# First attention of a four-layer model: order of scores and maxima products, place of the second batch's output turn, and six score banks in the last group

## The reference, cut to what matters

```python
qkv = jnp.einsum('bsd,od->bso', x, w_project)          # 16 heads of 16 features
att = jnp.einsum('bhqd,bhkd->bhqk', q, k) / math.sqrt(HEAD_DIM)
att = jnp.where(causal, -1e9, att)
att = jax.nn.softmax(att, axis=-1)
out = jnp.einsum('bhqk,bhkd->bhqd', att, v)
return jnp.einsum('bsd,od->bso', out.reshape(b, s, d), w_out)
```

## Time and profile before

| | |
|---|---|
| time, median of three runs | 1347.25 us |
| the profiled execution, its own time | 1347.06 us |
| its span | 1345.3 us |
| PE busy | 1225.4 us, 91% of the span |
| DVE busy | 731.3 us, 54% |
| ACT busy | 605.4 us, 45% |
| POOL busy | 121.5 us, 9% |
| first attention, first score to output projection | 85.65 to 182.60 us |

### The profile page before, as it was taken

How to read it: one execution, slowest core, us unless ns; L and a number is a source line. 1 busy time by engine, 2 the same in 40 slices (tenths; PEclk the granted TensorE clock), 3 DMA queues, 4 the chain that set the end, 5 groups by cost and what they waited for, 6 DMA issues and landing times.

```text
span 1345.3 us, 18762 instructions
## 1 busy us (share of the span) xinstructions
PE 1225.4 (91%) x6396; PEld 765.1 (57%) x6396; DVE 731.3 (54%) x2031; ACT 605.4 (45%) x1518; POOL 121.5 (9%) x144
## 2 busy tenths in 40 slices
PE   5988888888899889999999899999999999999994
PEld 4644444523277455656565687566666666667853
DVE  2777626836142578787878710444444444447257
ACT  2634553787623134545455402444545444442043
POOL 3230013432301300000000000000000000000000
PEclk9979999999999989999999999999999999999998
DMA  8001100230232400000000002100000000000000
GB/s 242 6 18 32 43 28 0 93 83 20 75 97 90 171 12 12 12 13 13 9 9 8 1 0 75 67 24 12 25 13 23 20 17 20 17 12 1 1 0 31
DMA packets 28046, 48.66 MB, mean 36 GB/s; under 512 B 3902, under 2 KB 22302, under 8 KB 26886
## 3 DMA queue, kind: packets, MB, share of 16 engines
q1 hardware_dynamic: 25222, 38.13, 8.8%
q0 software_dynamic: 2736, 9.37, 2.4%
HBM read 40.36 MB, written 9.19 MB: 37 GB/s over the span
## 4 chain that ended last, share of the span: by engine, by line
PE 69%; DVE 13%; issue 10%; ACT 7%; POOL 1%; DMA 0%; SPq 0%; ACTq 0%; POOLq 0%; DVEq 0%
PE bank L977 13%; PE bank L993 9%; PE bank L984 8%; PE bank L962 5%; PE bank L970 5%; PE bank L988 4%; PE bank L1223 2%; PE bank L886 2%; PE bank L897 2%; ACT PT L1487 2%; PE bank L1314 2%; PE bank L1274 2%; PE bank L1241 2%; PE bank L816 1%; PE bank L1301 1%
## 5 line engine op out<-in xcount | busy, mean ns | idle before, releaser
L1368 ACT COPY R<-bank 128x512 f32<-128x512 f32 (+4 forms) x199 | 106.3, 550 | 314.7 <-PE bank L993 142.8
L2064 DVE CUSTOM_DVE_ANT_0 bank<-bank,mask_row 128x128 f32<-128x128 f32 (+3 forms) x256 | 126.9, 497 | 173.4 <-PE bank L984 171.0
L977 PE MATMUL bank<-XNT,W 128*128 128x512 f32 x416 | 201.4, 608 | 7.4 <-ACT R L1368 3.8
L1515 ACT ACTIVATE R<-bank,nm 128x128 f32<-128x128 f32 (+3 forms) x256 | 136.0, 531 | 111.1 <-DVE nm L2064 110.1
L984 PE MATMUL bank<-R 128*128 128x512 f32 (+3 forms) x384 | 134.3, 434 | 0.0
L977 PEld LDWEIGHTS bank<-XNT,W 128*128 128x128 f32 x416 | 75.4, 192 | 101.9 <-issue 93.1
L962 PE MATMUL bank<-W,R 128*128 128x256 f32 x576 | 125.3, 380 | 3.2 <-ACT R L1368 3.2
L962 PEld LDWEIGHTS bank<-W,R 128*128 128x128 f32 x576 | 109.1, 190 | 18.7 <-ACT R L1368 2.1
L988 PE MATMUL bank<-identf,R 128*128 128x128 f32 x640 | 112.4, 275 | 6.3 <-DVE R L2081 4.7
L993 PE MATMUL bank<-PT,R 128*128 128x128 f32 (+3 forms) x384 | 112.0, 435 | 5.6 <-ACT PT L1368 4.2
L1368 ACT COPY PT<-bank 128x128 f32<-128x128 f32 (+3 forms) x256 | 108.6, 426 | 15.3 <-PE bank L988 15.1
(11 more groups left out here) (278 smaller groups left out, 1815.0 us busy)
## 6 DMA issues: line engine op xcount, KB each, us to landing
W<-in_wq SPq DMA_DIRECT2D x32, 128.0 KB, 2.0
W<-in_wo SPq DMA_DIRECT2D x2, 2048.0 KB
W<-in_egu SPq DMA_DIRECT2D x1, 2816.0 KB
W<-in_wk SPq DMA_DIRECT2D x20, 128.0 KB, 2.1
W<-in_wv SPq DMA_DIRECT2D x20, 128.0 KB, 2.0
R<-xg SPq DMA_DIRECT2D x5, 512.0 KB, 4.6
yg<-R SPq DMA_DIRECT2D x5, 512.0 KB, 3.5
W<-in_wa SPq DMA_DIRECT2D x2, 1024.0 KB, 4.7
```

What stands on the lines that cost most here:

```text
L977: ins = mm(bank[:, :], wqkv23[:, s, c, :], XNT[:, c, b * SEQ:(b + 1) * SEQ], start=c == 0, stop=c == DC - 1)
L1368: return nc.scalar.copy(dst, src)
L1515: return fn(Pr[c][:, 0:n], PS[c][:, 0:n], ACT.Exp, scale=-1.0, bias=nm[:, c:c + 1], accum_out=esum[:, c:c + 1])
L2064: return dve.tensor_tensor_reduce(out=s[:, 0:n], in0=s[:, 0:n], in1=mask_row[:, SEQ - n:SEQ], scale=-1.0, scalar=-MASKED, op0=ALU.add, op1 ...
```

## The change

Scores are no longer issued step by step but by number up to a limit, `scores(upto)`. In groups 0 to 2, step w issues three heads of step w + 1, then maxima tiles 0 and 1, then the fourth head. The output turn of a group's second batch moves from the group's end to step 0 of the next group, behind the fourth head's scores (for group 2 to step 1 of the last group), and DVE's normalisation moves with it. Only the last group's own second batch is still turned at the end. In the last group the scores from step 1 on use six banks, 3, 5, 7, 1, 2, 0 in turn: the first three wait for the last reduction of the maxima, the others for the exponential six scores before. The turn of the last maxima moves to step 0 behind the scores, and ACT copies them ahead of the exponentials of step 1 instead of step 2.

```diff
--- before.py
+++ after.py
@@ -323,6 +323,12 @@
         OUT_BANK, TURN_BANK = 4, 6
         MAX_BANKS = (3, 5, 7)
 
+        LAST0 = ((NG - 1) * B * TPB + 1) * GH
+        LAST_BANKS = (3, 5, 7, 1, 2, 0)
+
+        def score_bank0(n):
+            return n % 3 if n < LAST0 else LAST_BANKS[(n - LAST0) % 6]
+
 
         KV3_STEPS = {1: ("q", 0), 3: ("k", 0), 4: ("v", 0), 5: ("q", 1), 6: ("k", 1), 7: ("v", 1)}
         TILES = B * TPB
@@ -792,18 +798,26 @@
                 cb = coreb[0]
                 rows, stages = KQ + 3, B * TPB
 
-                def scores(g, w):
-                    b, j = w // TPB % B, w % TPB
-                    if j == 0:
-                        pe.wait_ge(nm_row[b], 64 * (g + 1 + B))
-                    q0 = j * P
-                    for h in range(GH):
-                        n = (g * stages + w) * GH + h
-                        pe.wait_ge(cb["pb_ready"], n + 1 + GH - 3)
-                        dst = PS[n % 3]
+                issued = [0]
+
+                def scores(upto):
+                    for n in range(issued[0], upto):
+                        g, w, h = n // (stages * GH), n // GH % stages, n % GH
+                        b, j = w // TPB, w % TPB
+                        if j == 0 and h == 0:
+                            pe.wait_ge(nm_row[b], 64 * (g + 1 + B))
+                        q0 = j * P
+                        if n < LAST0:
+                            pe.wait_ge(cb["pb_ready"], n + 1 + GH - 3)
+                        elif n < LAST0 + 3:
+                            pe.wait_ge(smax_used, NG * stages * TPB + 2)
+                        else:
+                            pe.wait_ge(cb["pb_ready"], n + 1 + GH - 6)
+                        dst = PS[score_bank0(n)]
                         mm(dst[:, q0:SEQ], kstk[0:rows, g * GH + h, b * SEQ + j * P:b * SEQ + (j + 1) * P],
                            qstk[0:rows, g * GH + h, b * SEQ + q0:(b + 1) * SEQ], start=True, stop=False)
                         mm(dst[:, q0:q0 + P], identb[:, :], mask_kq[:, :], start=False, stop=True).then_inc(cb["st_ps"], 1)
+                    issued[0] = max(issued[0], upto)
 
                 def values(g, w):
                     b, j = w // TPB, w % TPB
@@ -817,19 +831,20 @@
                                  PT[:, w % 2, h, q0:SEQ], start=j == 0, stop=j == TPB - 1)
                     ins.then_inc(cb["pv_ps"], 1)
 
-                def turn_outputs(g, b, last):
+                def turn_outputs(g, b, turned):
 
                     unit = g * B + b
                     pe.wait_ge(cb["oe_ready"], unit + 1 + 1)
                     pe.wait_ge(cb["otok_done"], unit + 2)
-                    pe.wait_ge(nm_sb, unit + (1 if last and b == 1 else 2))
+                    pe.wait_ge(nm_sb, turned)
                     for t in range(TPB):
                         ins = tr(PS[TURN_BANK][:, t * P:(t + 1) * P], OE[b][:, t * P:(t + 1) * P], identf[:, :])
                     ins.then_inc(cb["tk_ps"], 1)
 
                 def body(g, last):
                     for w in range(stages):
-                        if w == 1:
+                        nxt = (g * stages + w + 1) * GH
+                        if w == 1 and not last:
                             pe.wait_ge(cb["otok_done"], g * B + 2)
                             pe.wait_ge(nm_sb, g * B + 1)
                             turn_maxima(g, 1)
@@ -837,20 +852,27 @@
                             pe.wait_ge(cb["otok_done"], g * B + 1 + 2)
                             pe.wait_ge(nm_sb, g * B + 2)
                             turn_maxima(g + 1, 0)
-                        if w + 1 < stages:
-                            scores(g, w + 1)
-                        elif not last:
-                            scores(g + 1, 0)
                         if not last:
+                            scores(nxt + GH - 1)
                             max_scores(g + 1, w, (0, 1))
+                            scores(nxt + GH)
+                        elif w + 1 < stages:
+                            scores(nxt + GH)
+                        if w == 0 and last:
+                            pe.wait_ge(cb["otok_done"], g * B + 1)
+                            pe.wait_ge(nm_sb, g * B + 1)
+                            turn_maxima(g, 1)
+                        if w == 0 and g > 0 and not last:
+                            turn_outputs(g - 1, 1, g * B + 1)
+                        if w == 1 and last:
+                            turn_outputs(g - 1, 1, g * B + 2)
                         if w == TPB:
-                            turn_outputs(g, 0, last)
+                            turn_outputs(g, 0, g * B + 2)
                         if not last:
                             max_scores(g + 1, w, (2,))
                         values(g, w)
                         if not last:
                             max_scores(g + 1, w, (3,))
-                    turn_outputs(g, 1, last)
 
                 pe.sem_inc(cb["pv_ps"], 2)
                 pe.sem_inc(cb["tk_ps"], 2)
@@ -864,9 +886,10 @@
                         turn_maxima(0, 0)
                 pe.wait_ge(smax_used, B * GH * TPB + 2)
                 pe.wait_ge(const_made, 3)
-                scores(0, 0)
+                scores(GH)
                 for g in range(NG):
                     body(g, g == NG - 1)
+                turn_outputs(NG - 1, 1, NG * B)
 
             def attention1():
 
@@ -1464,7 +1487,7 @@
                 copy_maxima(0, 0)
                 for g in range(NG):
                     for w in range(B * TPB):
-                        if w == 2:
+                        if w == (1 if g == NG - 1 else 2):
                             copy_maxima(g, 1)
                         if w == TPB + 2 and g < NG - 1:
                             copy_maxima(g + 1, 0)
@@ -1473,7 +1496,7 @@
                         for h in range(GH):
                             n = (g * (B * TPB) + w) * GH + h
                             act.wait_ge(cb["st_ps"], n + 1)
-                            fn(PT[:, w % 2, h, q0:SEQ], PS[n % 3][:, q0:SEQ], ACT.Exp, scale=HD ** -0.5)\
+                            fn(PT[:, w % 2, h, q0:SEQ], PS[score_bank0(n)][:, q0:SEQ], ACT.Exp, scale=HD ** -0.5)\
                                 .then_inc(cb["pb_ready"], 1)
 
             def attention1():
@@ -2009,6 +2032,8 @@
                     for w in range(B * GH):
                         if maxima:
                             row_maxima(g + 1, w, (0, 1))
+                        if w == 0 and g > 0:
+                            normalise(0, g * B - 1, 1, g - 1)
                         if w == GH:
                             normalise(0, g * B, 0, g)
                         if maxima:
@@ -2017,7 +2042,7 @@
                             store_outputs(0, g * B + w // TPB)
                         if maxima and w % GH == GH - 1:
                             maxima_parts(g + 1, w // GH)
-                    normalise(0, g * B + 1, 1, g)
+                normalise(0, NG * B - 1, 1, NG - 1)
 
             def attention1():
```

## The result

The changed kernel took 1336.28 us in the median of eight runs (1334.84 to 1340.95), the kernel before 1346.79 us beside it (1344.97 to 1351.85). The ratio is 0.9923, with a 95% interval of 0.9907 to 0.9939, so the gain is 8 to 12.5 us. The forecast was 1336.0, from 1331 to 1341.5.

What follows compares the result with a forecast made beforehand. PE's order was taken to set the pace, with PE standing still inside it. Order 4.9, output turn 3.1 and last group 3.1 sum to 11.1 us, so 1347.06 - 11.1 = 1336.0 us, range 1331 to 1341.5.

Steps and rivals of the forecast that it cites:

- Part 1, order: Groups 0 to 2: fourth head's scores behind two maxima products save 0.78 us in each of six half groups; 4.9 us.
- The very first step: First step of the first attention, at half clock and without an output turn: given a saving of 0.2 us.
- 1.54 us of waits: PE's waits ahead of the fourth head's scores, steps 0 to 3 of a half group: 0.35, 0.48, 0.35, 0.36.
- No new DMA wait: Maxima rows of the next batch still arrive before PE's first scores, with 0.12 us left: loss taken as 0.
- bare chain: Last group, maxima turn to scores through ACT copy and four DMAs: 4.87 us, taken for the other groups too.
- 0.61 us of spare time: Other groups: PE takes 5.48 us from maxima turn to scores, against 4.87 for the DMA chain.
- rival A: Maxima rows come late in every half group, chain 5.48 us: saving 8.2, time 1338.9; chance 0.17.
- Part 2, output turn: Ends of groups 0 and 1: 2.03 us removed, 0.48 added in the next first step; 3.1 us for two.
- Part 3, last group: Last group: 2.0 us from the earlier maxima turn, net 1.1 behind the second batch's scores; 3.1 us.
- B: Every wait in half groups and at group ends goes, plus 4 in the last group: 17.9 us, 1329; chance 0.07.
- C: PE, arriving earlier, waits on DVE's three banks; only group ends and last group gain, 3.1+3.1: 1340.9; chance 0.12.
- D: Clock falls; last group and output projection run at half clock, costing up to 14 us: 1350, slower; chance 0.04.

Runs made afterwards that it cites:

- undoing run: Changed kernel with all four heads' scores of a step issued ahead of the two maxima products again: 1337.36 us, ratio 0.9957 to the kernel before.
- copy-first run: Changed kernel with DVE copying a unit's outputs ahead of the last reduction of the maxima instead of behind it: 1335.74 us, ratio 0.9893 to the kernel before.
- order alone: Kernel before with only the interleaved order of scores and maxima products, output turns and last group as before: 1344.83 us, ratio 0.9957 to the kernel before.

## Why the prediction was right

**Part 1, order (forecast 4.9, measured 4.4).** Steps 1 and 3 gave 0.29 each, as forecast, step 2 0.16 instead of 0.19, the steps with a turn nothing. The very first step gave nothing instead of 0.2: from its first 384-column score to the maxima turn it took 3.97 us before (87.76 to 91.73) and 3.98 after (84.38 to 88.36). The undoing run confirms 0.73 a half group. That the saving stops where another engine's result is next was the part of the working that mattered: the 1.54 us of waits promised twice as much. The copy-first run showed that DVE's copy takes it in steps 0 and 4: with the copy early, 0.34 of a step's 0.35 came back.

**No new DMA wait (forecast 0, measured 0.5).** The step that failed is that the bare chain of the last group, 4.87 us, holds for every unit. Five of the six chains fit in the 5.03 that PE now takes from the maxima turn to the scores. The maxima rows that the last group's first scores need take 5.48 to 5.82 in each of the eleven profiles in which PE comes early enough to notice. The 0.61 us of spare time that the earlier trace rows gave was measured on another unit, and the forecast that a DMA wait shows in the last group only came out otherwise: it stands ahead of that group too. The price of rival A was right for one unit of six; its mechanism isn't the broadcasts.

**Part 2, output turn (forecast 3.1, measured 3.1).** Group end and first step together took 2.03 + 3.24 before and take 3.73 now, 1.54 less, twice.

**Part 3, last group (forecast 3.1, measured 3.2).** The size was right, and so were the moments in it: 1.9 us came up to the second batch's scores (L+9.14 to L+7.25, forecast 2.0) and 1.3 behind them (forecast 1.1). Behind them the gain is the six banks': with three it takes 10.82 from there to the projection (18.14 - 7.32), with six 9.53. The banks cost 0.4 ahead of them (L+7.70 against L+7.32), where step 1's scores wait for the last reduction.

The attribution of the 2.0 to the early maxima turn doesn't hold. What had held the maxima turn until L+4.27 was the group end ahead of it as much as its own place, and either edit frees most of it. With the output turn moved and nothing else changed in the last group, the maxima turn comes at L+2.45 (156.64 - 154.19) and the group takes 18.14: 1.8 less than before. With the last group's own edits and no moved turn it takes 17.42: 2.6 less. Both together give 3.2, not 4.4, so 1.2 us are brought by whichever edit is there, and neither undoing shows them.

4.4 + 3.1 + 3.2 - 0.5 = 10.2, the stage's 10.19. Against the forecast of 11.1 the stage is 0.9 short; that the time came within 0.3 us of the forecast is luck of the other stages.

**The rivals.** A happened in one unit of six, and not by the broadcasts that spoke for it. B and C fall by the step lengths. D didn't happen in the changed kernel (1.00 in both windows above), and did, small, in the order alone.

## What to carry to other kernels

Where an in-order engine waits for a bank, work that needs neither the bank nor its reader can go into the wait; but the saving ends at the next thing that is late, so list, for each step, the moment of every release: after the edit the next-latest one sets the start, and that gives the gain. When several edits touch one stretch, undo each by itself and also compare them with the kernel that has none: here 1.2 us came with either of two edits, and undoing one at a time showed them in neither. A spare time of 0.6 us measured on one unit is no proof for its neighbours.

## What the runs showed of the hardware

- A chain of four small DMAs took 5.48 to 5.82 us in the eleven profiles in which an instruction load started ahead of the last packet of the fourth, and at most 5.03 in the units without one. Where the load started behind the row (4.81 us after the maxima turn, in two profiles), PE came at 5.47 and 5.48 without a DMA wait.
- The clock went to half for about 3 us in the order-alone kernel after a stretch in which PE was busy for 0.62 of 2.00 us, in both of its profiles. The kernel before, in which PE stands still for the same 1.38 us at each group end, kept full clock.
- From the first maxima turn on, two profiles of one kernel agreed to 0.03 us (80.68 and 80.69, 78.55 and 78.52), where the whole time of one kernel spreads over 5 to 11 us in six to ten runs. The start of the stage repeats less well: 5.67 to 6.25 us, with the time that the granted clock was 0.50. The two profiles of the order alone differ by 0.38 (87.42 and 87.80), nearly all of it in the DMA wait.
